# Gated cross-attention layer with a blockwise FFN: router mask and bias moved from TensorE to VectorE, row maxima carried with later queries

## The reference

```
q = layernorm(x)                       # per token, 256 features
att = softmax(causal(q k^T / 4)) v     # k = v = ctx, 16 heads of 16 features
x = x + tanh(g_xattn) * att
xn = layernorm(x)
prob = softmax(xn @ w_router + b_router)           # 16 blocks
mask = 1 for the 4 likeliest blocks, else 0        # per token
h = relu(xn @ w1^T + b1)               # 1024 = 16 blocks of 64
y = (h * mask of the block) @ w2^T + b2
x = x + tanh(g_ffn) * y
```

## Time and profile before

| | |
|---|---|
| median of 3 executions | 814.26 us (813.39 to 815.47) |
| the profiled execution | 814.01 us, of which the span of the trace is 812.3 us |
| TensorE busy | 772.9 us (95%) |
| VectorE / ScalarE / GpSimd busy | 533.4 / 366.2 / 343.0 us |
| mean DMA rate | 36 GB/s |

### The profile page before, as it was taken

The page is one execution under the profiler, slowest core; times in us unless marked ns, Lnnn a source line. Parts: engine busy times, 40 slices in busy tenths (PEclk is TensorE's granted clock), DMA queues, the critical chain, the costliest instruction groups (busy, mean ns, idle before and its releaser), DMA issues.

```text
span 812.3 us, 26057 instructions
## 1 busy us (share of the span) xinstructions
PE 772.9 (95%) x11232; PEld 654.2 (81%) x11232; DVE 533.4 (66%) x1460; ACT 366.2 (45%) x748; POOL 343.0 (42%) x550
## 2 busy tenths in 40 slices
PE   4676899999999999999999999999999999999898
PEld 3554689798888979888887978888897888888687
DVE  4465776676667667766776676667667676766432
ACT  1455444535454453444445444544544445353411
POOL 4799644334433433443344344334433443433200
PEclk9779999999999999999999999999999999999999
DMA  4020101101010100111010011101010110000000
GB/s 138 28 80 29 30 28 54 28 16 43 33 50 29 54 30 16 41 42 42 29 54 29 19 38 42 41 29 54 29 38 19 42 41 29 28 3 16 14 27 27
DMA packets 29707, 29.64 MB, mean 36 GB/s; under 512 B 2573, under 2 KB 29325, under 8 KB 29594
## 3 DMA queue, kind: packets, MB, share of 16 engines
q1 hardware_dynamic: 29594, 27.98, 10.7%
HBM read 19.04 MB, written 8.39 MB: 34 GB/s over the span
## 4 chain that ended last, share of the span: by engine, by line
PE 89%; POOL 6%; DVE 3%; issue 1%; ACT 1%; DMA 0%; SPq 0%; DVEq 0%; POOLq 0%
PE bank L237 8%; PE bank L270 8%; PE bank L375 8%; PE bank L376 8%; PE bank L377 7%; PE bank L349 7%; PE bank L351 7%; PE bank L283 7%; PE bank L350 7%; PE bank L215 4%; PE bank L358 4%; PE bank L296 3%; PE bank L223 3%; PE bank L307 3%; PE bank L243 2%; PE bank L257 1%
## 5 line engine op out<-in xcount | busy, mean ns | idle before, releaser
L674 POOL TENSOR_SCALAR_AFFINE_SELECT weights<-weights 128x1024 f32<-128x1024 f32 x128 | 138.1, 1103 | 141.4 <-ACT weights L437 141.4
L518 DVE TENSOR_REDUCE neg_max<-bank 128x4 f32<-128x512 f32 x256 | 158.7, 682 | 21.8 <-PE bank L243 21.8
L375 PE MATMUL bank<-w_high,h_high 128*128 128x256 f32 x512 | 154.1, 301 | 1.0 <-DVE h_low L572 1.0
L437 ACT ACTIVATE weights<-bank 128x512 f32<-128x512 f32 x256 | 132.3, 603 | 47.2 <-PE bank L270 47.2
L660 POOL TENSOR_SCALAR ve<-mv 128x1 f32<-128x1 f32 x128 | 30.4, 237 | 274.7 <-DVE mv L502 274.6
L377 PE MATMUL bank<-w_high,h_low 128*128 128x256 f32 x512 | 144.4, 282 | 0.0
L376 PE MATMUL bank<-w_low,h_high 128*128 128x256 f32 x512 | 144.3, 282 | 0.0
L457 ACT ACTIVATE h_high<-bank 128x512 fp32r<-128x512 f32 x128 | 76.5, 597 | 101.8 <-PE bank L358 101.8
L349 PE MATMUL bank<-xT_high,w_high 128*128 128x512 f32 x256 | 111.6, 436 | 1.0 <-DVE h_low L572 1.0
L572 DVE SCALAR_TENSOR_TENSOR h_low<-bank,h_high 128x512 fp32r<-128x512 f32 x128 | 84.7, 681 | 38.0 <-ACT h_high L457 38.0
L531 DVE RECIPROCAL gain<-bank 128x16 f32<-128x16 f32 x64 | 16.5, 258 | 140.3 <-PE bank L296 140.2
(11 more groups left out here) (89 smaller groups left out, 1258.5 us busy)
## 6 DMA issues: line engine op xcount, KB each, us to landing
c_in<-in_ctx SPq DMA_DIRECT2D x32, 256.0 KB, 2.9
x_in<-in_x SPq DMA_DIRECT2D x32, 256.0 KB, 3.1
out_y<-y_out SPq DMA_DIRECT2D x32, 256.0 KB, 2.3
w_stage<-in_w1T SPq DMA_DIRECT2D x1, 1024.0 KB, 8.3
qT<-maxT SPq DMA_DIRECT2D x64, 8.0 KB
w_stage<-in_w2T SPq DMA_DIRECT2D x1, 1024.0 KB, 5.8
b_all<-in_b SPq DMA_DIRECT2D x1, 128.0 KB, 3.7
select<-b_parts SPq DMA_DIRECT2D x4, 6.0 KB
```

What stands on the lines that cost most here:

```text
L375: pe.matmul(out=bank[:, 0:D], lhsT=h_high[:, c, toks], rhs=w2_high[:, c, :], start=a, stop=False)
L437: act.activation(weights[:, b % 2, u * HB:(u + 1) * HB, :].rearrange("p h q -> p (h q)"), banks[SCORE_BANK[u]][:], ACT.Exp, scale=SCALE).t ...
L518: dve.tensor_reduce(out=neg_max[:, b % 2, u * HB:(u + 1) * HB], in_=banks[SCORE_BANK[u]][:].rearrange("p (h k) -> p h k", h=HB), axis=AX_X ...
L674: pool.affine_select(out=w, in_=w, compare_op=ALU.is_ge, fill=0.0, base=0, pattern=[[0, 2 * HB], [1, S]], channel_multiplier=-1).then_inc( ...
```

## The change

1. The four score banks become one PSUM tensor. The row maximum is one reduce over 128x2048, and it writes its result into a spare column (`RIDE_COL`) of the padded queries of batch b+2. It is turned with them, so `max_transposed` and the copy `maximum_rows` are gone. SP's DMA now copies four rows within `qT`, from the slot of batch b+2 to that of batch b, in the same iteration in which it is needed.
2. The transposed queries move from the second place of TensorE's list to its end (of the batch i+3), and from bank 6 to bank 7. Two more of them run at the end to carry the last maxima.
3. The exponentials are two operations of 128x1024 where there were four of 128x512.
4. The `select` products and the table are gone, and the splitting of b1 with them. The mask (now 1 where a block is chosen) is turned by four transposes at the end of R's attention work, copied by VectorE to `usedT` (16 partitions, one for each block), and spread by eight DMAs to `used_all`: DMA c copies two partitions of `usedT` to 64 partitions each.
5. VectorE computes `hid` = (bank + b1) * mask from the bank. ScalarE makes the high part from `hid` in SBUF and then takes the relu of `hid` in place, two operations for each chunk. GpSimd subtracts (`hidden_low`), which was VectorE's work.

```diff
 def q_transposed(b):                      # now last in the iteration, for i+3
-    if b >= 5:
-        pe.wait_ge(xT_high_made, b - 4)
+    if b >= MAX_LAG:
+        pe.wait_ge(max_found, b - MAX_LAG + 1)
+    if b >= 4:
+        pe.wait_ge(att_made, b - 3)
...
 def hidden(g, c):
     if c >= 2:
-        pe.wait_ge(h_low_made, HC * g + c - 1)
+        pe.wait_ge(hid_made, HC * g + c - 1)
...
-    for t in range(GROUP):
-        made = pe.matmul(out=bank[:, t * S:(t + 1) * S], lhsT=select[:, t, cols],
-                         rhs=unusedT[:, gs, :], start=False, stop=t == GROUP - 1)
...
 def ffn_piece(i, n):                      # ScalarE
-    act.wait_ge(hidden_made, HC * g + c + 1)
-    act.activation(h_high[:, c, :], banks[FFN_BANK[c % 2]][:], ACT.Relu).then_inc(h_high_made, 1)
+    act.wait_ge(hid_made, HC * g + c + 1)
+    act.activation(h_high[:, c, :], hid[:, c % 4], ACT.Relu)
+    act.activation(hid[:, c % 4], hid[:, c % 4], ACT.Relu).then_inc(hid_clipped, 1)
...
 def ffn_piece(i, n):                      # VectorE
-    dve.wait_ge(h_high_made, HC * g + c + 1)
-    dve.scalar_tensor_tensor(h_low[:, c, :], banks[FFN_BANK[c % 2]][:], 0.0, h_high[:, c, :].bitcast(F32),
-                             ALU.max, ALU.subtract).then_inc(h_low_made, 1)
+    dve.wait_ge(hidden_made, HC * g + c + 1)
+    if c == 0:
+        dve.wait_ge(used_landed, 16 * HC * (g + 1))
+    if HC * g + c >= 4:
+        dve.wait_ge(h_low_made, HC * g + c - 3)
+    dve.scalar_tensor_tensor(hid[:, c % 4], banks[FFN_BANK[c % 2]][:], b1_cols[:, c:c + 1], used_all[:, c],
+                             ALU.add, ALU.mult).then_inc(hid_made, 1)
...
+def hidden_low(i, n):                     # GpSimd, pieces 0 and 1 before causal_weights, 2 and 3 behind it
+    pool.wait_ge(hid_clipped, HC * g + c + 1)
+    pool.tensor_tensor(h_low[:, c, :], hid[:, c % 4], h_high[:, c, :].bitcast(F32),
+                       ALU.subtract).then_inc(h_low_made, 1)
...
 def max_row(b):                           # SyncE, in iteration b; was in iteration b - 1
-    s = b % TS
-    sync.wait_ge(max_copied, b + 1)
-    sync.dma_start(qT[MAX_COL::PAD, s, :].rearrange("u (r t) -> u r t", t=S), maxT[:, b % 2, :]).then_inc(max_landed[s], 16)
+    s, ride = b % TS, b + MAX_LAG
+    sync.wait_ge(q_copied, ride + 1)
+    sync.dma_start(qT[MAX_COL::PAD, s, :], qT[RIDE_COL::PAD, ride % TS, :]).then_inc(max_landed[s], 16)
...
+def used_rows(g):                         # SyncE, in R, behind max_row and the loads
+    sync.wait_ge(used_copied, g + 1)
+    for c in range(HC):
+        blocks = usedT[c * P // BLOCK:(c + 1) * P // BLOCK]
+        sync.dma_start(used_all[:, c], blocks.unsqueeze(1).to_broadcast([P // BLOCK, BLOCK, GROUP * S])
+                       ).then_inc(used_landed, 16)
```

More of the change, by code:

```diff
@@ L56, in sem @@
             return ctx.enter_context(nc.semaphore(name))
-        banks = [ctx.enter_context(nc.psum_tensor(f"bank{i}", [P, BANK], F32)) for i in range(BANKS)]
+        score_banks = ctx.enter_context(nc.psum_tensor("score_banks", [P, U, BANK], F32))
+        banks = [None] * U + [ctx.enter_context(nc.psum_tensor(f"bank{i}", [P, BANK], F32)) for i in range(U, BANKS)]
         ident = sb("ident", [P, P], F32)
@@ L324, in logits_transposed, with used_transposed @@
                 pe.transpose(banks[M1][:, 0:P], logitT[:], ident[:]).then_inc(route_turned, 1)
-            def unused_transposed(g, i):
+            def used_transposed(g):
                 bank = banks[M1][:].bitcast(BF16)
-                pe.wait_ge(unused_made, g + 1)
-                if i - 1 <= N:
-                    pe.wait_ge(att_made, i - 1)
-                pe.transpose(bank[:, 0:S], unused[:].rearrange("p t e -> p (t e)"),
-                             ident16[:]).then_inc(unused_turned, 1)
+                pe.wait_ge(used_made, g + 1)
+                for t in range(GROUP):
+                    turned = pe.transpose(bank[:, t * S:(t + 1) * S], used[:, t], ident16[:])
+                turned.then_inc(used_turned, 1)
             def hidden(g, c):
@@ L418, in _ @@
                     x_transposed(i - 2)
+                if g is not None:
+                    used_transposed(g)
                 ffn_piece(i, 2)
@@ L435, in exponentials @@
                 act.wait_ge(rescored, b + 1)
-                for u in range(U):
-                    act.activation(weights[:, b % 2, u * HB:(u + 1) * HB, :].rearrange("p h q -> p (h q)"),
-                                   banks[SCORE_BANK[u]][:], ACT.Exp, scale=SCALE).then_inc(exp_done, 1)
+                for half in range(2):
+                    act.activation(weights[:, b % 2, half * 2 * HB:(half + 1) * 2 * HB, :].rearrange("p h q -> p (h q)"),
+                                   score_banks[:, 2 * half:2 * half + 2].rearrange("p u n -> p (u n)"),
+                                   ACT.Exp, scale=SCALE).then_inc(exp_done, 1)
             def out_copied(b):
@@ L784, in _ @@
                     load(b // PAIR)
-                if i == GROUP + 1:
-                    sync.wait_ge(select_made, 3 * GROUP)
-                    sync.wait_ge(b1_split, 1)
-                    for t in range(GROUP):
-                        row = PAD * t + BLOCKS
-                        sync.dma_start(select[row:row + PARTS, t, :],
-                                       b1_parts[:].rearrange("o a n -> o (a n)")).then_inc(b1_landed, 16)
+                g = router_group(i)
+                if g == 0:
+                    sync.wait_ge(w_low_made, 8)
+                if g is not None:
+                    used_rows(g)
                 g, phase = ffn_phase(i)
```

208 lines of the change are left out of this document (85 added, 123 removed).

## The result

| | before | changed |
|---|---|---|
| median of the runs on one chip | 814.59 us (4 runs) | 1462.3 us (1458.24 to 1466.5, 4 runs) |
| ratio, 95% interval | | 1.795 (1.790 to 1.801) |
| profiled execution, its span | 814.0, 812.3 us | 1458.24, 1456.5 us |
| predicted | | 1165 (1050 to 1270) |

The direction was right and the size was not: the kernel lost 644 us where 351 were forecast, outside the range.

What follows compares the result with a forecast made beforehand. TensorE was taken as the bound. To 814 us it added 34 for late helpers, 299 for the mask by DMA and 27 for the clock, less 8 at the start: 1166, rounded to 1165 us, range 1050 to 1270.

Steps and rivals of the forecast that it cites:

- TensorE is the bound before; 2.7 us a group to gain: On TensorE, dropped select products and turned maximum save 2.7 us a group, 43 us in all, if nobody is late.
- The chain of VectorE and ScalarE ahead of the keys: VectorE's and ScalarE's work on `hid` delays the keys' copy, so TensorE waits: 2.1 us a group, 34 us in all.
- Two engines, eight DMAs one after the other on the same two: Mask transfer: each DMA uses two of 16 engines, all eight the same two, 23.5 us in sequence; stall 299 us in all.
- The second rival: The mask DMAs spread over engines and cost at most 1.8 us a group; 850 us for the kernel, chance 0.14.
- 46 ns for a row: Mask transfer: each 1 KB row takes 46 ns on one DMA engine, with 40 to 58 as ends.
- the sign: Sign of a wrong forecast: a mask row taking 35 or 60 ns puts the size off by 90 us or more.
- Clock: After each group's TensorE stall the clock halves for 3.4 us, losing 1.7 us; 27 us in all, ends 0 and 54.
- The start: At the kernel's start, GpSimd's table leaves the chain, saving 8 us, with ends 5 and 20.
- Rival 1: TensorE stays the bound and all waits hide; 763 us for the kernel, chance 0.03.
- Rival 3: The maximum row's DMA comes 2 us late in each of 64 iterations, without stacking of mask DMAs; 968 us, chance 0.02.

Runs made afterwards that it cites:

- e12: e8 with a semaphore for each of the eight mask DMAs, so VectorE's product of a chunk waits for that chunk's mask alone; 798.53 us, ratio 0.981.
- e4: The changed kernel without the mask DMAs, `used_all` set to ones once, so the choice of blocks is left out; 864.69 us, ratio 1.060.
- e6: e2 with the 8 copies of each block's mask row placed 8 partitions apart instead of adjacent; 892.25 us, ratio 1.090.
- e8: e6 with ScalarE's whole queue ordered by what TensorE wants next and GpSimd's second-norm rstd moved up; 806.29 us, ratio 0.990.
- e7: e6 with ScalarE's copy of the keys put ahead of the two Relu passes of piece 0; 885.68 us.
- e2: The changed kernel with each block's mask row on 8 adjacent partitions and every mask DMA reading 16 partitions; 931.13 us, ratio 1.143.

## Why the prediction failed, point by point

- **TensorE is the bound before; 2.7 us a group to gain.** The bound is right, the gain was too large. In e12, where hardly anybody is late, TensorE is busy 35 us less than before, where the forecast had 43, and a steady group takes 46.30 us instead of 44.4. TensorE is idle for 1.0 of these 1.9 us, most of it for `h_low` in C and `hid` in A, and busy for 45.26 where 44.4 were forecast. In windows from row maximum to row maximum the busy time falls by 1.72 us in A and B together (forecast 2.34), by 0.23 in C (0.21), and it grows by 0.10 in R, where a fall of 0.13 was forecast. The rows don't say where the 0.6 us in A and B went.
- **The chain of VectorE and ScalarE ahead of the keys.** Right in kind. In e4, whose steady groups show this term without the mask's transfer, A takes 12.34 us (forecast 12.3), B 13.75 (13.2), C 11.82 (11.8) and R 12.03 (11.88). The sum was 2.1 us a group and is 2.86: 12 us more in 16 groups, most of it in B. The listed releasers are the named ones, the copies of the keys (44.1 us in 34 waits, where two waits of 1.6 in each group make 51) and of the attention output (23.9 us in 16).
- **Two engines, eight DMAs one after the other on the same two.** Right. The DMA share is 0.13 while nothing but the mask moves, and the landing fits a sum of 512 rows on each of two engines; which two of the 16 they are, no row shows. The trace before had no two narrow DMAs at once, so that half rested on a choice, which held. The second rival, that they spread (850 us), did not happen. e6, where they were made to spread, gives 892; e4, with no transfer at all, is already at 865.
- **46 ns for a row.** This is the step that failed. The figure came from a load from DRAM over all 16 engines, and the upper end of 58 ns from a single short burst; for the lower end of 40 no row stands. In none of these did two engines read the state buffer through one port for long. The row took 80 ns. The mask landed 43.0 us after its first issue, where 24.9 were forecast. `usedT` was ready 0.8 us sooner than forecast (605.83 - 597.17 = 8.7), so that the mask came 39.6 us into A instead of 22.5: 17.1 us more in each group, 274 in all. A rate read where the rows came from DRAM was carried to two engines that read neighbouring partitions of the state buffer, without an upper end for sharing; twice 46 was the end that the range lacked. The text had named the sign ("if a row takes 35 or 60 ns, the size is off by 90 us or more") and left 80 out.
- **Clock.** The mechanism was right. In the group shown the granted clock was 0.50 (1.2 GHz) from about 619 to 656.5 us, and TensorE resumed at 651.4: 5.1 us at half speed, 2.5 lost, where 1.7 were forecast.
- **The start.** 8 us were forecast. The eighth row maximum begins at 74.70 us against 83.08, so 8.4 were gained.
- **Rows that add up.** The sum forecast 1166. The row time adds 274, the clock 13 and the helper chain 12: 1465, against 1458 measured. The group taken is one of the longer ones: A lasts from 48.9 to 51.2 us, 49.95 in the mean, which makes the sum 1453. The remaining 5 us are not accounted for.
- **Rival 1, TensorE stays the bound (763 us).** Its two conditions, a mask by 3.8 us into A and keys in time, are needed, and meeting them nearly (e8) or for each chunk (e12), by spread sources and another order, gives 806 and 799. They aren't enough for 763: the 36 us left in e12 are mostly the 1.9 us a group of the first point.
- **Rival 3, the maximum row late.** It does not appear. TensorE waited for that row twice in the whole run, 41.6 us in all. One of the two waits, 35.9 us, is as long as the mask's stall, and the row's DMA stands behind the mask's on SyncE. A wait in each of 64 iterations, as the rival had it, there wasn't.

## What to carry to other kernels

A rate of the DMA engines is a rate of a transfer's sources and engines together: before a small tile is spread by broadcasting, write down which partitions each DMA reads at once, and put replicas of it on partitions with different ports (here partitions 1 or 32 apart moved 25 to 32 GB/s, partitions 4, 8 or 64 apart 46 to 48). Removing work from the bound engine is worth what the helpers' queues allow. The same changed work took 892 us in one order of ScalarE and GpSimd and 806 in another, so read for each copy in an in-order queue when its consumer wants it, and put the passes that nobody waits for last. When a wait vanishes and the time stays, look for the next copy behind it in the same queue, as in e7.

## What the runs showed of the hardware that was not expected

- Two DMA engines reading partitions 1 or 32 apart moved 25 to 32 GB/s together; 4, 8 or 64 apart, 46 to 48 GB/s; from DRAM 46.
- The issue of a DMA on SyncE is not always 0.54 us. With two engines at work, the first two of the eight mask DMAs took SyncE some 0.6 us each and the last five about 5 us each (29.5 us for all), and the store and the maximum row behind them waited as well. With 16 engines eight issues took 5.1 to 6.6 us, median 0.60 to 0.67 each.
- With 16 source partitions the same 1 MB moved at 112 to 191 GB/s when these were adjacent (e2) and at 201 to 203 GB/s when they were 8 apart (e6), by windows of 2 us inside the transfer.
- ScalarE's passes of 128x512 from the state buffer to itself follow each other every 0.53 us (starts at 651.23 and 651.76 in the changed kernel) while each is recorded as 0.61 to 0.63 us long: the pitch, not the length, is the price in a queue.
